# Two-layer graph network with expert layers on one core: the first stage weighs the relation sums of two batches by one matmul call

## What is computed

```
edge_index: src, dst (206250 edges, sorted by dst); relation 0..7 and weight for each edge
msg = layernorm(x)[src] * weight
agg = segment_sum(msg, relation * N + dst)      # 8 relations
x   = x + sum over r of blockdiag(W_r) applied to agg_r
...   # then experts of two (layer 0), a graph attention layer, and dense experts (layer 1)
```

## Time and profile before

| what | value |
|---|---|
| median of 3 runs | 5944.67 us (5944.37 to 5950.27) |
| profiled execution | 5958.87 us, its span 5956.8 us |
| mean granted TensorE clock | 0.791 |
| PE / PEld busy | 4136.2 / 3330.2 us |
| DVE / ACT / POOL busy | 1657.3 / 1082.2 / 3178.3 us |
| first stage, roughly | 102 to 2860 us |
| gathers of the first stage | 1588 on L695, 946 ns each |

### The profile page before, as it was taken

One profiled execution on the slowest core, in us unless ns is written; L12 is line 12 of the kernel. 1 busy time (PEld: TensorE's weight loads), 2 busy tenths in 40 slices (PEclk: granted clock), 3 DMA queues, 4 the chain that ended last, 5 costly groups with the idle time before them and its releaser, 6 DMA issues. The chain is left out here.

```text
span 5956.8 us, 65813 instructions
## 1 busy us (share of the span) xinstructions
PE 4136.2 (69%) x20734; PEld 3330.2 (56%) x20734; DVE 1657.3 (28%) x5503; ACT 1082.2 (18%) x2144; POOL 3178.3 (53%) x3331
## 2 busy tenths in 40 slices
PE   1666666666666666666997267777777777777778
PEld 1665565656665656566886145554555455455546
DVE  5232322323222323233566011111121111112112
ACT  2010110101010101011564011121122112122212
POOL 5555555555555555553222665655555565556551
PEclk7777777777777777777998577877887787788779
DMA  5222222222222222221112433333333333333331
GB/s 170 73 83 84 83 83 85 80 86 80 85 81 83 82 83 83 83 82 54 59 48 68 133 94 99 96 93 98 96 98 91 98 97 94 96 96 100 92 97 42
DMA packets 223401, 522.56 MB, mean 88 GB/s; under 512 B 59660, under 2 KB 93918, under 8 KB 223332
## 3 DMA queue, kind: packets, MB, share of 16 engines
q0 software_dynamic: 155392, 430.52, 26.1%
q1 hardware_dynamic: 35768, 44.79, 2.4%
q10 hardware_dynamic: 32172, 46.39, 2.3%
HBM read 475.24 MB, written 46.24 MB: 88 GB/s over the span
## 5 line engine op out<-in xcount | busy, mean ns | idle before, releaser
L695 POOL DMA_INDIRECT ring<-xn,index x1588 | 1501.9, 946 | 1165.9 <-ACT index L708 693.1
L1697 POOL DMA_INDIRECT ring<-table,index x1616 | 1543.3, 955 | 1071.5 <-ACT index L1712 606.3
L814 PE MATMUL bank<-spare,ring 128*128 128x160 f32 x6448 | 1059.2, 328 | 265.4 <-issue 182.2
L814 PEld LDWEIGHTS bank<-spare,ring 128*128 128x128 f32 x6448 | 1022.9, 215 | 289.2 <-issue 217.7
L1892 PE MATMUL bank<-ring,acc 128*32 128x264 f32 x3232 | 577.6, 544 | 470.2 <-issue 415.0
L1766 ACT ACTIVATE ework<-bank,bn 128x256 f32<-128x256 f32 x800 | 406.5, 560 | 1506.2 <-remote 998.1
L824 PE MATMUL bank<-cells,wblk 128*128 128x128 f32 x1632 | 396.7, 365 | 399.2 <-issue 392.5
L1892 PEld LDWEIGHTS bank<-ring,acc 128*32 128x32 f32 x3232 | 187.5, 137 | 798.6 <-issue 774.0
L824 PEld LDWEIGHTS bank<-cells,wblk 128*128 128x128 f32 x1632 | 320.5, 262 | 467.5 <-issue 464.9
L1913 PE MATMUL bank<-acc,wa 128*128 (+1 forms) x1600 | 500.0, 463 | 90.9 <-ACT acc L1757 65.5
L824 PE MATMUL bank<-spare,wblk 128*128 128x128 f32 x1600 | 340.0, 355 | 286.9 <-issue 284.4
(11 more groups left out here) (272 smaller groups left out, 3019.9 us busy)
## 6 DMA issues: line engine op xcount, KB each, us to landing
ring<-table,index POOLq DMA_INDIRECT x1616
ring<-xn,index POOLq DMA_INDIRECT x1612
sums<-acc ACTq DMA_DIRECT2D x101, 132.0 KB
acc<-sums ACTq DMA_DIRECT2D x25, 264.0 KB
table<-frow SPq DMA_DIRECT2D x24, 264.0 KB, 3.0
nx<-in_x ACTq DMA_DIRECT2D x24, 256.0 KB
x<-nx ACTq DMA_DIRECT2D x24, 256.0 KB
fx<-x SPq DMA_DIRECT2D x24, 256.0 KB
```

Of the source, the lines that this page charges most:

```text
L695: pool.indirect_dma_start(ring[:, m * BT + t, :], None, k.xn_d, bass.IndirectOffsetOnAxis(ap=index[m][:, t:t + 1], axis=0)).then_inc(got[m ...
L814: ins = pe.matmul(win[q][:, h, :], ring[:, m * BT + q * QUAD + t, h * P:(h + 1) * P], onehot[:, (q * QUAD + t) % HELD, :], start=(t == 0), ...
L1697: pool.indirect_dma_start(ring[:, par * BT + t, :], None, k.table1_d, bass.IndirectOffsetOnAxis(ap=index[par][:, t:t + 1], axis=0)).then_i ...
```

## The change

The cells of the four batches are laid out in two pairs, (m = 1, m = 2) in one array and (m = 3, m = 0) in the other. The weighing runs only in periods of odd m, over the pair b - 2 and b - 1: for each half and relation one call of 2 x 128 columns instead of two calls of 128; the first one (b = 1) covers batch 0 alone with 128 columns. The window bank is used whole (512 columns). DVE waits once for a pair and makes two window adds in the odd periods, after the fourth quad's add. ACT clears both cells in the odd periods, after `done`. ACT's index cast of batch b + 3 no longer waits for a weighing; it waits for `summed` to reach 4b, that is for all quads of batch b - 1. The last weighing (batches 99 and 100) runs in the period after the last batch, where before batch 99 was weighed one period earlier.

```diff
--- before.py
+++ after.py
@@ -631,8 +631,9 @@
         a = allocator(nc, ctx)
         ring, index = k.ring, k.index
         size = H * RELS * (P + NEAR)
-        flat = [a.sb(f"cells{m}", [P, size])[:] for m in range(2)] + [k.spare[:, m * size:(m + 1) * size]
-                                                                     for m in range(2)]
+        pairs = [v.rearrange("p (u c n) -> p u c n", u=2, n=P + NEAR)
+                 for v in (a.sb("cells", [P, 2 * size])[:], k.spare[:, 0:2 * size])]
+        flat = [pairs[i][:, u, :, :].rearrange("p c n -> p (c n)") for i, u in ((1, 1), (0, 0), (0, 1), (1, 0))]
         cells = [v.rearrange("p (c n) -> p c n", n=P + NEAR) for v in flat]
         rest = k.spare[:, 2 * size:]
         onehot = rest[:, 0:HELD * CELLS].rearrange("p (t c) -> p t c", t=HELD)
@@ -646,7 +647,7 @@
         ln.var, ln.rstd, ln.tmp = (a.sb(f"n{n}", [P, PAIR]) for n in ("var", "rstd", "tmp"))
         banks = [a.bank(f"bank0_{i}", BANK) for i in range(7)]
         win = [banks[q][:, 0:H * CELLS].rearrange("p (h c) -> p h c", h=H) for q in range(QUADS)]
-        window_ps = banks[4][:, 0:H * P].rearrange("p (h n) -> p h n", h=H)
+        window_ps = banks[4].rearrange("p (h u n) -> p h u n", h=H, u=2)
         columns = sums[:].rearrange("f h (t p) -> f h t p", t=PAIR)
         rows_ps = banks[6].rearrange("p (t d) -> p t d", t=PAIR)
         turn_ps = banks[5].rearrange("p (h t n) -> p h t n", h=H, t=PAIR)
@@ -747,13 +748,16 @@
                     stage_scal(b + 2, (m + 2) % 4)
                 if on_chip and mine and p == NORM0:
                     keep_columns(j)
-                if window:
-                    act.wait_ge(done, b)
                 if gathers and later:
+                    if not (isinstance(b, int) and b == 0):
+                        act.wait_ge(summed, QUADS * b)
                     stage_index(b + 3, (m + 3) % 4)
-                if window:
-                    act.copy(cells[(m - 1) % 4], zero[:].unsqueeze(1).broadcast_to([P, H * RELS, P + NEAR])
-                             ).then_inc(cleared, 1)
+                if window and m % 2:
+                    act.wait_ge(done, 2 * n + (m + 1) // 2)
+                    for u in (2, 1):
+                        if not (isinstance(b, int) and b < u):
+                            act.copy(cells[(m - u) % 4], zero[:].unsqueeze(1).broadcast_to(
+                                [P, H * RELS, P + NEAR])).then_inc(cleared, 1)
                 if mine and p == TURN0:
                     store(j)
                 if mine and p == PLACE:
@@ -816,13 +820,15 @@
                 ins.then_inc(summed, 1)
 
             def weigh(b, m):
+                first = isinstance(b, int) and b == 0
                 pe.wait_ge(added, QUADS * b + quads_of(b))
-                if not (isinstance(b, int) and b == 0):
-                    pe.wait_ge(windowed, b)
+                if not first:
+                    pe.wait_ge(windowed, b - 1)
                 for h in range(H):
                     for r in range(RELS):
-                        ins = pe.matmul(window_ps[:, h, :], k.wblk[:, h, r, :], cells[m][:, h * RELS + r, 0:P],
-                                        start=(r == 0), stop=(r == RELS - 1))
+                        both = pairs[1 if m == 0 else 0][:, :, h * RELS + r, 0:P]
+                        ins = pe.matmul(window_ps[:, h, 1, :] if first else window_ps[:, h, :, :], k.wblk[:, h, r, :],
+                                        both[:, 1, :] if first else both, start=(r == 0), stop=(r == RELS - 1))
                 ins.then_inc(done, 1)
 
             def fetch(j):
@@ -848,7 +854,7 @@
                         quad(b, m, n, q)
                     if on_chip and mine and p == NORM0 and q == 1:
                         fetch(j)
-                    if window and q == (0 if isinstance(b, int) and b == BATCHES - 1 else 2):
+                    if window and m % 2 and q == 2:
                         weigh(b - 1, (m - 1) % 4)
                 if mine and p == TURN0:
                     turn(j)
@@ -905,15 +911,14 @@
                     return (b, m, q + 2) if q + 2 < quads_of(b) else None
                 return None if isinstance(b, int) and b == BATCHES - 1 else (b + 1, (m + 1) % 4, q + 2 - QUADS)
 
-            def add_window(b):
+            def add_window(b, u):
                 _, base = nc.values_load_multi_w_load_instructions(
                     k.base16[0:1, cols(b, 1)], engines=[dve.engine], min_val=0, max_val=COLS - P - AHEAD0,
                     skip_runtime_bounds_check_because="a node's number is below N")
-                dve.wait_ge(done, b + 1)
                 if not (isinstance(b, int) and b == 0):
                     dve.wait_ge(windowed, b)
                 here = k.acc[:, :, cols(base[0] + AHEAD0, P)]
-                dve.tensor_tensor(here, here, window_ps, ALU.add).then_inc(windowed, 1)
+                dve.tensor_tensor(here, here, window_ps[:, :, u, :], ALU.add).then_inc(windowed, 1)
 
             def add(b, m, q, bases):
                 if q == 0 and not (isinstance(b, int) and b < 4):
@@ -961,8 +966,11 @@
                             add(b, m, q, bases)
                             if ahead:
                                 one_hots(*ahead)
-                if window:
-                    add_window(b - 1)
+                if window and m % 2:
+                    dve.wait_ge(done, 2 * n + (m + 1) // 2)
+                    for u in range(2):
+                        if not (isinstance(b, int) and b < 2 - u):
+                            add_window(b - 2 + u, u)
                 if mine and p == NORM0:
                     norm(j, on_chip)
```

## The result

The changed kernel takes 6273.82 us (median of 4 runs, 6268.18 to 6276.21), the kernel before 5946.73 beside it: 1.055 times as long, 95% interval 1.0538 to 1.0563, or 327 us more. The forecast was 6048 within 5825 to 6210: the direction was right, the size too small by more than two thirds, and the time lies above the range. The loss lies in the range of the prediction's rival 2 (+216 to +350 us).

What follows compares the result with a forecast made beforehand. Bound: a loop of waits, PE's completions arriving late while POOL streams gathers. A round of four periods goes from 107.0 to 111.5 us, +108 over 24 rounds, with once-only parts +103: about 6048 us, whole range 5825 to 6210.

Steps and rivals of the forecast that it cites:

- rival 2: First stage: both pairs of periods run as double streams of gathers, +216 to +350 us, about 6220 us; chance 0.10.
- The mechanism: First stage: while POOL streams gathers, PE's completions reach others late, later in longer streams; a stream ends at 1.40 us per gather.
- The two periods from m = 2: Casts of m = 2 to m = 0: one stream of 32 gathers, then weighing and clears, 50.5 to 60.8 us, taken as 55.6.
- the cast from m = 0 to m = 1: Even period without a weighing: the fourth sum after a cast decides the next cast, at 23.9 us instead of 26.75.
- m = 1 to m = 2: Period with weighing: stream end 23.9, fourth quad at low clock 4.4, then 3.7 to the end of the copy: 32.0 us.
- The column copy and window adds ahead of the m = 2 cast: In ACT's and DVE's queues: these end 3.7 us behind the fourth quad, with the second window add taken as 0.8.
- The two clears: ACT, odd periods: two clears of 2.16 us behind `done` put the next cast 4.6 us after it, 4.3 plus 0.3.
- The weighing of 32 matmuls: PE: a pair of 256 columns takes 6.8 us at clock 1.00, 13.7 at 0.50; no gain in PE's time proper.
- rival 4: PE's weighing: loads cost time of their own, so halving them saves 163 us, giving 5782 us; chance 0.03.
- streams that stay apart: Rival 1, first stage: no double streams form, -22 to -154 us a run, about 5850 us; chance 0.32.

Runs made afterwards that it cites:

- e4b: Kernel before without the first stage's gathers after the fourth batch (output not the reference's): 4752.49 us, on a chip where the kernel before takes 5945.67.
- e1b: Changed kernel with the index cast waiting for summed 4b + 3 instead of 4b: 5852.11 us, ratio 0.984 to the kernel before, at 5945.67 on that chip.
- e1: Changed kernel with the index cast waiting for summed 4b + 3 instead of 4b, on the chip of 4683 us: 4686.96 us, ratio 1.001 to the kernel before.
- e2: Kernel before with only the early index cast, weighings of one batch kept, on the chip of 4683 us: 4681.80 us, ratio 0.9997.
- e3: Kernel before with the early cast, and POOL's gathers of a quad waiting for the sum three batches back instead of four: 4682.83 us, ratio 1.000.
- e8: Kernel before with gathered rows of 128 values instead of 256 after the fourth batch: 6069.47 us, beside 6057 to 6070 for the kernel before.

## Why the prediction was wrong

**The mechanism was right** for a chip with late sums. That sums come late while POOL streams, and the more so the longer the stream, carried the forecast; e4b shows that the gathers are the cause, e1b that the double streams are the loss. 32 gathers at 1.40 us each put the end of the lateness at 1037.88 + 44.8 = 1082.7; DVE's add came at 1083.43.

**The two periods from m = 2** were forecast at 55.6 us, in the middle of 50.5 to 60.8. They took 1093.64 - 1036.81 = 56.8, and 57.1 on average over the stage.

**The step that failed is the cast from m = 0 to m = 1**, put at 23.9 because "the fourth sum after a cast decides, and that comes at +23.9". It came at +13.4 (1093.64 to 1107.03; 13.2 on average over the stage). In the kernel before, the first sum after a cast (+2.9) is that of the quad behind the weighing. In the changed kernel the cast waits for this very quad, and for the clears besides; PE goes on meanwhile, and the sums after the cast are at +0.9, +2.8, +5.3 and +13.4. So the fourth sum falls where the third fell before (+15.4), not where the fourth did. The cast of m = 1 then comes while POOL's 16 gathers run, and its own 16 follow without a stop. I had seen this for m = 2, where the copy delays the cast more, and for m = 0 only in rival 2, at a chance of 0.10, though its condition ("one quad more is through") follows from numbers that I had: two clears of 2.16 us behind `done` against 2.2 us for the fourth quad. They measured 4.2 and 2.3 us.

**m = 1 to m = 2**, forecast at 32.0 with a stream of 16, fell with it: 50 us, as the second half of a double stream. A round took 120.3 us on average (57.1, 13.2 and 50.1) instead of 111.5: 8.8 us more in each of 24 rounds, 211 of the 224 us between the forecast's +103 and the measured +327. Rival 2 had twice 60.8 = 121.6.

**Smaller terms.** The column copy and window adds ahead of the m = 2 cast were put at 3.7 us behind the fourth quad's sum; they took 1036.81 - 1033.64 = 3.2. The two clears took 4.23 for 4.3. The weighing of 32 matmuls from 1023.45 took 7.88 us, for 6.8 in columns at the full clock: the granted clock was 0.77 from 1023.5 to 1027 and 1.00 behind that. In one piece no time was won by the width as such. The rule in rival 4 (the Trainium skill, page "TensorE: Matmul & The Clock Gate", section "Back-to-back issue gap") would have given some 100 us less; e1b, with all wide calls and mostly single streams, is 94 us below before. But e1b also has an even period without a weighing, so this doesn't show that the width itself saved it, and at the full clock the trace has the time of the columns alone.

**Range and chances.** A third of the chance was on faster, by streams that stay apart. That case exists: it is e1b, at 5852 where 5850 was written. It needed a wait that the change had taken out. That the two figures are so close is in part luck, since e1b's rounds are built otherwise (mostly three casts 24.0 us apart and one 30.1, where the rival had 23.9 twice, 28.5 and 29.8).

## What to carry to other kernels

A wait that looks like a needless dependence can be what paces a producer. Before it is moved forward, ask what the producer does with the time: here 16 more gathers at once, during which the sums of the engine that is to use them come late. When the fourth event after a release decides, count the events anew for each kind of period, from the new release. A pace by quads, tied to the sums themselves (one line in POOL's queue), was worth 3.6% with the early cast, more than the 1.6% of the pair weighing with its wait moved. All of this holds where sums are late; on the chip of 4683 us none of e1 to e3 made a difference of more than 0.1%.

## What the runs showed of the hardware

- While POOL issues indirect gathers without a stop (one in 1.25 us), the semaphore increments of PE's matmuls can reach the other engines long after the matmuls are recorded: 14 us in a stream of 16, 36 us in one of 32 (recorded until 1047.44, seen at 1083.43). The last late sum of a stream comes 4.1 us after the start of the last gather in the first case (1043.38 and 1047.48) and 6.1 us in the second (1077.38 and 1083.43). With the gathers taken out a sum comes 0.14 us after its quad (e4b). No run tells whether the matmuls themselves ended late, their recorded ends being modelled, or only their increments.
- Halving each gathered row (DMA from 83 to 43 GB/s, 32 packets a gather instead of 48) changed nothing in that (e8).
- It depends on the chip, or on what else differed between the runs on it: the kernel before took 4683, 5945 and 6062 us on different ones, and on the first POOL's gathers alone set the period, 20.1 us (e2). Why chips differ is open, and so is what in a gather holds up PE's increments.
- The trace names a gather ("DMA ring") as what ended DVE's wait for a late sum (595.6 us in 40 waits in the changed kernel). The semaphore waited for was PE's.
